# Matmuls whose results nobody reads, put into the lead-in of the second attention

## The reference, cut to what matters

```python
q = (x @ wq).reshape(B, T, N_HEADS, HEAD_DIM)       # B = 2, T = 1024, 32 heads of 16
k = x @ wk
v = x @ wv
scores = jnp.einsum('bqhd,bkd->bhqk', q, k) * scale
scores = jnp.where(causal[None, None], scores, -jnp.inf)
probs = jax.nn.softmax(scores.astype(jnp.float32), axis=-1).astype(x.dtype)
out = jnp.einsum('bhqk,bkd->bqhd', probs, v).reshape(B, T, C)
```

## Time and profile before

| | us |
|---|---|
| median of 3 runs | 2147.05 |
| lowest, highest | 2145.66, 2149.94 |
| the profiled execution, own time | 2148.23 |
| its span, first to last instruction | 2146.4 |
| PE busy | 1964.6 (92%) |
| DVE busy | 1174.6 (55%) |
| ACT busy | 903.1 (42%) |

### The profile page before, as it was taken

How to read it: one execution, slowest core, us unless ns; L and a number is a source line. 1 busy time by engine, 2 the same in 40 slices (tenths; PEclk the granted TensorE clock), 3 DMA queues, 4 the chain that set the end, 5 groups by cost and what they waited for, 6 DMA issues and landing times. The chain is left out here.

```text
span 2146.4 us, 34674 instructions
## 1 busy us (share of the span) xinstructions
PE 1964.6 (92%) x12824; PEld 1177.3 (55%) x12824; DVE 1174.6 (55%) x2557; ACT 903.1 (42%) x1909; POOL 524.5 (24%) x408
## 2 busy tenths in 40 slices
PE   4859999999999999999986899997999999999698
PEld 4635666666666666666643454553444444444377
DVE  3536655555555555555401454446676767765078
ACT  2513344444444444444440122221666656656444
POOL 0014245555434444555330000000000000000143
PEclk8969999999999999999998999996999999999799
DMA  9742233222333233322236221144132222210121
GB/s 308 272 143 60 61 80 81 62 58 58 76 81 80 71 80 80 80 60 57 66 93 198 69 69 48 51 111 134 22 53 42 38 52 39 42 37 19 33 88 59
DMA packets 113594, 172.21 MB, mean 80 GB/s; under 512 B 26186, under 2 KB 46826, under 8 KB 113298
## 3 DMA queue, kind: packets, MB, share of 16 engines
q1 hardware_dynamic: 112402, 169.75, 29.8%
q10 hardware_dynamic: 1024, 0.26, 0.1%
HBM read 84.32 MB, written 29.38 MB: 53 GB/s over the span
## 5 line engine op out<-in xcount | busy, mean ns | idle before, releaser
L890 ACT ACTIVATE at_prob<-at_scp 128x512 f32<-128x512 f32 (+1 forms) x608 | 349.8, 576 | 515.4 <-PE at_scp L993 514.4
L1663 ACT ACTIVATE as_prob<-as_scp 128x512 f32<-128x512 f32 (+2 forms) x640 | 308.7, 564 | 197.5 <-PE as_scp L1773 148.2
L925 DVE CUSTOM_DVE_ANT_0 at_junk<-at_mxp,causal 128x128 f32<-128x128 f32 (+3 forms) x512 | 243.5, 488 | 190.5 <-PE at_mxp L1004 185.7
L1713 DVE TENSOR_REDUCE as_mxd<-as_mxp 128x2 f32<-128x256 f32 (+3 forms) x256 | 202.6, 820 | 98.3 <-PE as_mxp L1792 96.1
L920 DVE TENSOR_REDUCE at_mxf<-at_mxp 128x1 f32<-128x512 f32 x256 | 176.0, 688 | 143.4 <-PE at_mxp L1004 139.6
L1698 POOL TENSOR_TENSOR l_att_t<-l_att_t,as_spread 64x1024 f32<-64x1024 f32 x16 | 37.9, 2368 | 860.3 <-DMA as_spread<-l_recips 860.3
L820 POOL TENSOR_TENSOR at_pre<-at_prob 128x512 f32<-128x512 f32 x64 | 80.1, 1281 | 410.6 <-ACT at_prob L890 410.6
L1711 DVE TENSOR_REDUCE as_mxf<-as_mxp 128x2 f32<-128x1024 f32 x128 | 151.0, 1221 | 52.8 <-PE as_mxp L1787 52.6
L820 POOL TENSOR_TENSOR at_pre<-at_pre,at_prob 128x512 f32<-128x512 f32 x128 | 160.5, 1284 | 3.6 <-ACT at_prob L890 1.2
L1817 PE MATMUL as_op<-as_prob,l_vn 128*32 128x512 f32 (+3 forms) x1536 | 158.1, 533 | 0.3 <-ACT as_u_sb L1670 0.3
L989 PE MATMUL at_scp<-hd_early_q,l_khi 97*128 97x512 f32 (+1 forms) x304 | 138.3, 455 | 11.3 <-DMA hd_late_q<-at_slo 8.2
(11 more groups left out here) (250 smaller groups left out, 3494.4 us busy)
## 6 DMA issues: line engine op xcount, KB each, us to landing
hd_late_q<-at_slo SPq DMA_DIRECT2D x96, 128.0 KB, 2.4
at_qhi<-at_shi SPq DMA_DIRECT2D x96, 128.0 KB, 2.5
at_qlo<-at_slo SPq DMA_DIRECT2D x96, 128.0 KB, 2.4
hd_early_q<-at_shi SPq DMA_DIRECT2D x84, 128.0 KB, 2.4
at_spread<-l_recips SPq DMA_DIRECT2D x64, 128.0 KB, 2.7
l_o<-at_u_sb SPq DMA_DIRECT2D x16, 512.0 KB, 3.4
hd_early<-in_wmod SPq DMA_DIRECT2D x7, 1024.0 KB, 6.8
hd_late<-l_o SPq DMA_DIRECT2D x12, 512.0 KB, 4.1
```

The source lines that it names most:

```text
L890: nc.scalar.activation(prob[:, x % RING0, c0:HALF], scp[x % BANKS0][:, c0:HALF], ACT.Exp).then_inc(s["exp_done"], 1)
L925: nc.vector.tensor_tensor_reduce(out=junk[:, u % 2, 0:w], in0=tile[:, 0:w], in1=k.causal[:, HALF - w:HALF], scale=1.0, scalar=LOWEST, op0= ...
L1663: nc.scalar.activation(prob[:, x % RING1, cols], scp[x % BANKS1][:, cols], ACT.Exp).then_inc(s["exp_done"], 1)
L1713: nc.vector.reduce_max(mxd[:, t % 2, :, i, qt:qt + 1], tile[:, :, 0:(qt % 4 + 1) * P], AX_X).then_inc(s["mx_done"], 1)
```

## The change

Behind each of the 32 maxima of the lead-in PE gets two more matmuls of 48 rows and 512 columns, one for each row group, and behind the first turning sixteen more (`UNREAD` pairs of two). They read the first query tile and the keys, and write to the score tiles `scp[0]` and `scp[1]`, which the first scores overwrite. They wait for nothing and signal nothing. That is 80 matmuls in all. The loop behind the lead-in, the other engines and the transfers stay as they are.

```diff
 LEAD = MSTEP + 8
+UNREAD = 8
...
+                def unread_ahead():
+                    for jj in range(2):
+                        rows = slice(RG * jj, RG * jj + MAXROW)
+                        nc.tensor.matmul(scp[jj][:], q[0][rows, 0, 0:P], k.keys[rows, 0, 0:HALF], start=True, stop=True)
+
...
                 for u in range(LEAD):
                     maximum(u)
+                    unread_ahead()
                 turn_maxima(0)
+                for _ in range(UNREAD):
+                    unread_ahead()
                 for g in range(QSETS):
```

## The result

The changed kernel takes 2149.79 us (median of 15 runs, 2146.9 to 2155.76), the kernel before 2146.06 us (median of 15 runs beside them, 2142.31 to 2149.94). The ratio is 1.0019 with a 95% interval of 1.0012 to 1.0027: slower by some 4 us, at the edge of what I had called measurable (0.2%), and inside the forecast range. It isn't the "no change" of the sum. Two single executions of later kernels, of 3563 and 2731 us, fell in a slower state and are left out of all times and ratios.

The account below looks back on a forecast made before the run. PE's work at full clock was taken to set the time nearly everywhere, with DVE fullest in mid lead-in. Terms +2.0 + 0.5 - 2.5 summed to 0.0 us, so 2147.1 us was forecast, range 2142.5 to 2152.0.

Parts of the forecast that it names:

- the sum: Whole kernel: +2.0 in the lead-in, +0.5 behind the turning, -2.5 in step 0, giving 0.0 us; chance 0.41.
- The price of a pair: Each added pair costs PE 0.44 us at half clock, 0.22 at full clock; bounds 0 and 0.80 us.
- The lead-in: Pairs behind the 32 maxima: between +3.0 and -2.1 us, taken as +2.0 with a clock rise in part at best.
- My walk for a low clock: Lead-in at half clock throughout: 1.2 us late at the ninth maximum, 0.9 in the middle, 0.9 at the end, +3.0.
- deduction of 1.0 for a rise on the way: Lead-in: clock expected to rise in a part of the small maxima at best, so +2.0 taken in place of +3.0.
- Behind the turning: Eight pairs in the 2.81 us wait for the row: 0.7 us late at half clock, hidden at full; taken +0.5.
- Step 0: Sets 0 to 4: full clock about a microsecond after the row wins 2.5 us; bounds 0 and -2.9.
- rival D: Steps: won and given back later, low stretches move, one more or fewer is 1.7 us, 2145.4 or 2148.8; chance 0.20.
- steps 1 to 14 keep 33.3 and 31.6 us: Loop behind step 0: steps 1 to 14 should keep their two lengths, 33.3 and 31.6 us.
- B: Lead-in and block: clock doesn't rise before 1509.2 and PE is late, +3.7 us, 2150.8 us; chance 0.20.
- C: Clock up in nearly the whole lead-in and from the first score on, -5.0 us, 2142.1 us; chance 0.13.
- E: Nothing happens: pairs all hidden, clock as before, 2147.0 us; chance 0.06.

Follow-up runs that it names:

- the block alone: Changed kernel without the pairs behind the 32 maxima, the sixteen matmuls behind the first turning kept; ratio 1.0002 to the kernel before.
- the filler over all rows: Changed kernel with each pair behind a maximum replaced by one fp32 matmul of 128 rows, 128 columns, sixteen matmuls behind the turning kept; ratio 1.0075.
- the pairs alone: Changed kernel without the sixteen matmuls behind the first turning, the pairs behind the 32 maxima kept; ratio 1.0014 to the kernel before.
- two-pair kernel: Changed kernel with two pairs behind each lead-in maximum in place of one; one execution, 2150.6 us, beside a median of 2147.8 for the kernel before.
- doubled pair: Kernel before, no lead-in filler, first matmul pair issued twice in maxima of sets 6 and 7 (2138.5 us against 2144.3, 0.9966) or sets 4 to 7 (1.0001).

## Why the prediction was right, and where its terms were off

**The price of a pair** (0.44 us at half clock, by columns) held: the block's eight pairs took 3.78 us with the last tail of some 0.35, 0.43 us a pair, and the lead-in took 35.0 us with 512 columns, 32.35 with 256 and 31.57 where only full maxima carry a pair.

**The lead-in** is the term that was mis-sized: I took +2.0 and it is +3.48. My walk for a low clock had +3.0: 1.2 at the ninth reduction (measured 1.27), 0.9 in the middle (measured 0.95), 0.9 at the end (measured 1.1), and 0.2 at the turning, which waits behind the last pair and which I had left out. What was wrong was the deduction of 1.0 for a rise on the way. There was none in any profile with one pair.

**Behind the turning** I took +0.5 and it is +0.55. **Step 0** to set 4: I took -2.5, it is -3.08, just past my bound of -2.9.

**What is missing in the sum** is rival D, to which I gave a chance of 0.20 and one stretch of 1.7 us. The gain was given back nearly in full: +1.6 in the rest of step 0, -1.6 in steps 1 to 13, +1.6 in step 14, +1.2 in step 15. Steps 0 to 14 have one low stretch more than before, and step 15 one more. I had also written that steps 1 to 14 keep 33.3 and 31.6 us; step 14 took 29.9 before and 31.5 after. It wasn't chance where the stretches fell. In all five profiles (both of the changed kernel, both of the block alone, and that of the filler over all rows) in which step 0 began at full clock behind a block of eight, the low stretches stand in the even steps, eight of them; in the kernel before and with the pairs alone they stand in the odd steps, seven of them. The two-pair kernel, which was at full clock earlier, has seven in the odd steps, so full clock at the start of step 0 alone doesn't decide it. That the low stretches come from thin PE work in sets 4 to 7 is made likely by the doubled pair: in sets 6 and 7 it leaves three of seven, and in sets 4 to 7 none of steps 0 to 14 that begins in those sets. It isn't shown beyond doubt, since the doubled pair also makes each step 0.3 or 0.7 us longer, and no run changes the length of a step without its density. What fixes the alternation isn't shown.

So 2.0 + 0.5 - 2.5 should have been 3.5 + 0.55 - 3.1 + 2.8 = +3.8 us. It stayed within the range because the two errors, 1.5 and 2.8 us, less the 0.6 us by which the term for step 0 was too cautious, came to less than the 4.9 us up to its end, and within 0.2% by a hair. That is the width of the range and some luck, not the sum: the sum had the loss and the gain cancel, and they didn't.

**Rivals.** B was half right: no rise in the lead-in and its price (+3.5 for my +3.0), but the block did raise the clock. That the result lies 1 us from B's 2150.8 is chance, since its parts differ. C didn't come: PE called busy for 13.1 of 13.2 us was at 0.50. E fell.
The Trainium skill (TensorE: Matmul & The Clock Gate, section "A second HAM failure mode: psum-queue depth-cycling") has short idles between groups of matmuls as what makes the clock go up and down. In this lead-in it didn't go up and down: with one pair behind each maximum it stayed at 0.50 for 35 us, and with two pairs it rose once, 25.7 us behind the first maximum, and stayed. So no run here shows that pattern in the lead-in.

## What to carry to other kernels

Matmuls that nobody reads cost what sticks out from behind the engine that sets the pace: behind the eight full maxima (two reductions in 2.35 us) a pair of 0.44 us was free in the lead-in, and the 24 pairs behind small or diagonal maxima, 10.6 us of PE work, cost 3.5 us. Look whether the clock rises behind them, and take them away where it doesn't. That they are placed in a wait or beside a fuller engine isn't enough: the block in the wait made nothing faster (1.0002), and the eight free pairs with it came out slower (1.0032), for a cause that stays open. And follow the gain to the end of the loop: 3.1 us won in the first step were gone by the last, because the low stretches moved; the version that put filler into sets 6 and 7 of the steps won 0.34%, some of it behind the attention, while twice as much filler won nothing and half as much lost 0.23%.

## What the runs showed of the hardware that I had not expected

- A PE that is called busy for 34.90 of 35.00 us (the pairs alone) stayed at 0.50 for the whole lead-in. The busy time counts tails of short matmuls: one of 512 columns is recorded at 0.79 us at half clock, while the eight pairs of the block took 0.43 us each.
- What followed the block went by whether PE still worked on it when the row came. In the five profiles in which it did (sixteen matmuls of 512 columns, 3.78 us), the clock was 1.00 within 0.7 us of the first score. In the three in which PE or its weight load waited for the row (twelve matmuls, 0.68 us; sixteen of 256 columns, 1.09 us; sixteen of 512 with the late row, 1.41 us), it stayed at 0.50 for another 10.9 to 13.6 us.
- In the kernels without filler in the steps the low stretches come in every second of steps 1 to 13, 33.3 and 31.6 us, and steps 0, 14 and 15 vary. They stand in the even steps where the clock rose at the first score, and in the odd ones where it rose with the first values or, with two pairs, well before the first score.
- Filler of half the width (256 in place of 512 columns in sets 6 and 7) made the kernel slower than none (1.0023); in its profile the clock was 0.53 over 25 us of the last step.
